# Halved value products in the self-attention, and a last batch whose expert results are written straight to token rows, in a three-part decoder layer on one core

## The reference, cut to what matters

```python
# x: (4, 512, 128) float32, ctx: (4, 154, 128), mask: (4, 1, 512, 154)
x = x + causal_attention(layernorm(x), Wk, Wq, Wv)              # one head of 128
x = x + cross_attention(layernorm(x), ctx, mask, wq, ..., bo)   # 16 heads of 8
x = x + block(layernorm(x))
def block(x):
    q, k, v = (x @ W + b for W, b in ...)                       # 16 heads of 8, rotary on q and k
    ao = softmax(q k^T / sqrt(8)) v                             # full 512 x 512, per head
    x1 = layernorm(x + ao @ Wo + bo) * g1 + be1
    p, e = top_k(softmax(x1 @ Wg + bg), 2)                      # 2 of 8 experts per token
    y = gelu(x1 @ W1[e] + b1[e]) @ W2[e] + b2[e]                # 128 -> 512 -> 128
    return layernorm(x1 + sum(p * y)) * g2 + be2
```

## Time and profile before

| | before |
|---|---|
| median of 3 executions | 735.01 us (733.05 to 737.16) |
| the profiled execution | 731.61 us, span 729.8 us |
| mean granted TensorE clock in it | 0.953 |
| TensorE matmul busy | 639.2 us, 88% |
| VectorE busy | 456.0 us, 62% |
| ScalarE busy | 344.2 us, 47% |
| GpSimd busy | 120.7 us, 17% |

### The profile page before, as it was taken

The page is one execution under the profiler, slowest core; times in us unless marked ns, Lnnn a source line. Parts: engine busy times, 40 slices in busy tenths (PEclk is TensorE's granted clock), DMA queues, the critical chain, the costliest instruction groups (busy, mean ns, idle before and its releaser), DMA issues.

```text
span 729.8 us, 10620 instructions
## 1 busy us (share of the span) xinstructions
PE 639.2 (88%) x3790; PEld 390.5 (54%) x3798; DVE 456.0 (62%) x1119; ACT 344.2 (47%) x617; POOL 120.7 (17%) x121
## 2 busy tenths in 40 slices
PE   4899899998898999999898999999889999887940
PEld 2564454346655753368636643388447533476840
DVE  4673688737934678458826678677436777378303
ACT  0405027773044457765244567763444566542520
POOL 5100100001041100001224200030406000220414
PEclk9999999999989999999999999999999998998985
DMA  6300000001043540003252630021345500036841
GB/s 196 112 0 1 1 0 1 1 1 36 1 149 97 156 135 1 1 1 114 68 169 67 179 98 1 1 57 50 101 144 160 160 0 1 30 96 194 280 109 43
DMA packets 45084, 54.95 MB, mean 75 GB/s; under 512 B 4347, under 2 KB 35433, under 8 KB 45033
## 3 DMA queue, kind: packets, MB, share of 16 engines
q1 hardware_dynamic: 43240, 50.61, 23.8%
q0 software_dynamic: 1792, 3.67, 1.6%
HBM read 46.73 MB, written 7.54 MB: 74 GB/s over the span
## 4 chain that ended last, share of the span: by engine, by line
PE 61%; DVE 22%; issue 6%; ACT 4%; POOL 3%; DMA 2%; SPq 1%; POOLq 0%; ACTq 0%; DVEq 0%
PE banks L1730 9%; PE banks L1371 5%; PE banks L1720 5%; PE banks L1385 5%; PE banks L1699 4%; DVE nm L1203 3%; DVE nm L1139 3%; PE banks L1348 3%; PE banks L1681 3%; PE banks L1622 2%; PE banks L1620 2%; DVE hat L893 2%; PE banks L1639 2%; POOL rstd L566 2%; PE banks L1633 2%
## 5 line engine op out<-in xcount | busy, mean ns | idle before, releaser
L1203 DVE TENSOR_REDUCE nm<-banks 128x1 fp32r<-128x512 f32 x256 | 160.3, 683 | 41.5 <-PE banks L1699 40.4
L846 ACT ACTIVATE px<-banks 128x1024 f32<-128x1024 f32 x128 | 126.4, 1023 | 47.1 <-PE banks L1720 46.7
L674 ACT ACTIVATE hT<-banks,wp 128x128 f32<-128x128 f32 x240 | 68.3, 370 | 78.2 <-PE banks L1371 78.1
L566 POOL TENSOR_TENSOR rstd<-ve,misc 128x4 f32<-128x4 f32 x19 | 19.5, 1027 | 457.9 <-DVE ve L887 457.9
L1699 PE MATMUL banks<-kst,qst 32*128 32x512 f32 x256 | 84.3, 499 | 1.6 <-ACT kst L819 0.8
L1730 PE MATMUL banks<-px,vf 128*32 128x512 f32 x512 | 73.4, 647 | 4.8 <-ACT ot L852 3.1
L1371 PE MATMUL banks<-xT,wp 128*128 128x128 f32 x480 | 69.6, 292 | 7.9 <-DMA wp<-in_experts 4.8
L1371 PEld LDWEIGHTS banks<-xT,wp 128*128 128x128 f32 x480 | 63.0, 203 | 15.3 <-issue 9.7
L1385 PE MATMUL banks<-wp,hT 128*128 128x128 f32 x480 | 67.2, 285 | 2.2 <-ACT hT L674 2.1
L1385 PEld LDWEIGHTS banks<-wp,hT 128*128 128x128 f32 x480 | 62.0, 201 | 3.8 <-ACT hT L674 2.6
L1720 PE MATMUL banks<-q2st,kst 32*128 32x512 f32 x256 | 59.3, 513 | 0.0
(11 more groups left out here) (273 smaller groups left out, 988.9 us busy)
## 6 DMA issues: line engine op xcount, KB each, us to landing
wp<-in_experts SPq DMA_DIRECT2D x60, 514.0 KB, 4.7
b2r<-in_L_ffn_b SPq DMA_DIRECT2D x60, 64.0 KB, 4.3
expert_rows<-xs SPq DMA_DIRECT2D x12, 256.0 KB, 5.2
xs<-expert_tokens SPq DMA_DIRECT2D x9, 256.0 KB, 3.0
msk<-in_mask SPq DMA_DIRECT2D x4, 308.0 KB, 3.0
xin<-in_x SPq DMA_DIRECT2D x4, 256.0 KB, 2.9
ot<-in_const_sel SPq DMA_DIRECT2D x1, 1024.0 KB, 5.3
out<-yg SPq DMA_DIRECT2D x4, 256.0 KB, 2.3
```

The source lines that it names most:

```text
L566: pool.tensor_tensor(rstd[:, n, :], ve[:, n, :], exponent, ALU.pow).then_inc(k[f"ln_rstd{n}"], 1)
L674: ins = act.activation(hT[:, n % 2, c * P:(c + 1) * P], bank[h_bank(p, i)][:, c * P:(c + 1) * P], ACT.Gelu, bias=wp[:, n % WSLOTS, 2 * FF ...
L846: act.activation(px[:, c % 2, 2 * i:2 * i + 2, :], banks[:, 4 + 2 * i:6 + 2 * i, :], ACT.Exp, scale=SCALE_H).then_inc(k["f_exp"], 1)
L1203: dve.tensor_reduce(nm[:, t, g, BLK * hh:BLK * hh + 1], bank[s1_bank(g, t, i)], AX.X, ALU.max, negate=True).then_inc(k["f_max"], 1)
```

## The change

Five edits.

1. `sums_of` takes a range of columns. In the chunks that also have `s1`, from (0, 1) to (2, 2) of every batch, ten in number, the value product is cut into two halves of 256 columns, one behind each pair of `s1`, so 40 products become 80 halves. In chunk 3 of groups 0 and 1 the first half stands before `q2`. The other products stay whole.
2. The 52 `keep_warm` matmuls in `s2` are 256 columns wide and no longer 512.
3. In `cross` of batches 1 to 3, `up(p, 1)` stands before the turn of the normalised rows.
4. Last batch, order: only the first group of tokens is placed before the first tile, the others behind tiles 1, 5 and 9. Three more weight slots lie in `px`, which the attention no longer needs, so eight tiles' weights are loaded ahead. The output store of batch 2 stands behind all of the last batch's weight loads. The last tile's result goes to the bank of the group before, and its bias is added by itself.
5. Last batch, results: three small operations on VectorE and eight indirect writes (`send_ids`, 4 bytes a row) note in memory which token row each slot belongs to. SyncE loads that table (`row_of`). Each tile of the last batch is then written by one indirect write (`send_rows`) from `ysb` to the token rows in `token_rows`: four before `finish(B - 2)`, eleven behind it. `keep_y` and the eight indirect reads go for this batch; four plain loads fetch the rows. The last two passes over the output are folded into the layer norm's (subtract the mean and scale by g2 before the power is there, multiply and add behind it), and the output is stored in two halves.

```diff
+def w_slot(n):
+    i = n - NT * (B - 1)
+    if i < 0:
+        return n % WSLOTS
+    return (*range(WSLOTS, WSLOTS + WMORE), *range(WSLOTS))[i % (WSLOTS + WMORE)]
...
@@ SyncE
-                if n >= WSLOTS:
-                    sp.wait_ge(k["y_part"], n - WSLOTS + 1)
+                if w_free(n):
+                    sp.wait_ge(k["y_part"], w_free(n))
...
-                    for i in range(WSLOTS):
+                    for i in range(YG):
                         load_expert(B - 1, i)
-                for g in range((NT - WSLOTS) // YG, NG):
-                    keep_y(p, g)
-            sp.wait_ge(k["out_ready"], B)
-            sp.dma_start(out[B - 1].rearrange("(t p) d -> p t d", p=P), outb).then_inc(k["out_stored"], 16)
+                    keep_y(p, NG - 2)
+                    for i in range(YG, WSLOTS + WMORE):
+                        load_expert(B - 1, i)
+                    keep_y(p, NG - 1)
+                    sp.wait_ge(k["xs_sent"], 16 * 2 * T * B)
+                    sp.dma_start(row_of[:], row_dram.rearrange("(s i) o -> s (i o)", s=P)).then_inc(k["slots_loaded"], 16)
...
+            for i in range(2):
+                sp.wait_ge(y_sent[i], 16 * sum(min(YG, NT - YG * g) for g in range(i, NG, 2)))
+            for t in range(T):
+                sp.dma_start(yg[:, :, t, :], yt_dram[0:2 * S].rearrange("(j t p) d -> p j t d", j=2, p=P)[:, :, t, :],
+                             ).then_inc(xs_in[t], 16)
...
@@ GpSimd
+            def send_rows(i):
+                g = i // YG
+                n = NG * (B - 1) + g
+                if i == 0:
+                    pool.wait_ge(k["slots_loaded"], 32)
+                if i % YG == 0 or i == NT - 1:
+                    pool.wait_ge(k["y_out"], n + 1 + (i == NT - 1))
+                pool.indirect_dma_start(yt_dram, bass.IndirectOffsetOnAxis(row_of[:, i:i + 1], 0),
+                                        ysb[:, n % 2, i % YG, :], None).then_inc(y_sent[g % 2], 16)
...
-            pool.wait_ge(k["g_slots"], B)
+            send_ids()
             fetch_tokens(B - 2)
+            for i in range(YG):
+                send_rows(i)
             finish(B - 2)
-            fetch_tokens(B - 1)
+            for i in range(YG, NT):
+                send_rows(i)
             rstd_of(4, B - 1)
...
@@ VectorE, add_biases of the last batch
+                    if p == B - 1 and g >= 2:
+                        dve.wait_ge(y_sent[n % 2], 16 * YG)
...
@@ TensorE
-                        keep_warm(1, 4)
+                        keep_warm(1, 4, S // 2)
...
+                            if g * T + c and ga < G:
+                                sums_of(g * T + c - 1, i * S // 2, (i + 1) * S // 2)
                             if c == T - 1 and i == 0 and g + 1 < G:
                                 q2(g + 1)
-                            if g * T + c and i == (ga >= G or c == T - 1):
-                                if g * T + c == 1:
-                                    pe.wait_ge(k["f_v"], b + 1)
-                                sums_of(g * T + c - 1)
+                            if g * T + c and ga >= G and i:
+                                sums_of(g * T + c - 1, 0, S)
...
             place_tokens(0)
-            place_tokens(1)
             for i in range(NT):
                 up(B - 1, i)
                 if i:
                     down(B - 1, i - 1)
-                if i in (YG - 2, 2 * YG - 2):
-                    place_tokens(i // YG + 2)
+                if i in PLACES_BEHIND:
+                    place_tokens(i // YG + 1)
             down(B - 1, NT - 1)
```

More of the change, by code:

```diff
@@ L202, in y_bank, with w_loads, w_free @@
     return Y_BANKS[(g - GROUPS_BEFORE_F) % 2] if p == B - 1 or p == B - 2 and g >= GROUPS_BEFORE_F else Y_BANKS[0]
+def w_slot(n):
[3 more added lines that the diff above has]
+    return (*range(WSLOTS, WSLOTS + WMORE), *range(WSLOTS))[i % (WSLOTS + WMORE)]
+def w_loads(n):
+    return sum(w_slot(m) == w_slot(n) for m in range(n + 1))
+def w_free(n):
+    return max([m + 1 for m in range(n) if w_slot(m) == w_slot(n)], default=0)
 def rank_bank(p):
@@ L387, in build @@
         y_back = [sem(f"y_back{t}") for t in range(T)]
+        y_sent = [sem(f"y_sent{i}") for i in range(2)]
         block = stack.enter_context(nc.Block())
@@ L401, in build, with weights @@
         X_HEAD_BANKS = (4, 1, 2, 3)
+        def weights(n, first, last):
+            i = w_slot(n)
+            if i < WSLOTS:
+                return wp[:, i, first:last]
+            first, last = [S + WP * (i - WSLOTS) + c for c in (first, last)]
+            return px[:].rearrange("p i h s -> p (i h s)")[:, first:last]
         def a_scores(t):
@@ L524, in _ @@
                         load_expert(p, i)
-                for i in range(WSLOTS, NT):
+                ahead = WSLOTS if p < B - 1 else WSLOTS + WMORE
+                for i in range(ahead, NT):
                     load_expert(p, i)
-                    done = i - WSLOTS + 1
-                    if done % YG == 0:
+                    done = i - ahead + 1
+                    if done % YG == 0 and p < B - 1:
                         keep_y(p, done // YG - 1)
@@ L862, in _ @@
                 gelus(B - 2, label)
[L863 to L867 removed]
+            tokens_turned(B - 1, (0,))
+            for i in range(NT):
+                gelus(B - 1, (i,))
+                if i in PLACES_BEHIND:
+                    tokens_turned(B - 1, (i // YG + 1,))
         @block.vector
```

143 lines of the change are left out of this document (99 added, 44 removed).

## The result

| | before | changed |
|---|---|---|
| median of 4 executions each | 734.03 us (731.56 to 737.16) | 710.1 us (704.46 to 713.1) |
| ratio, 95% interval | | 0.967 (0.960 to 0.974) |
| the profiled execution | 731.61 us, span 729.8 | 712.04 us, span 710.2 |
| mean granted TensorE clock in it | 0.953 | 0.958 |
| attention of the four batches | 66.0, 71.2, 70.2, 71.6 | 61.7, 67.2, 69.7, 63.9 |

The attention runs from a batch's first `s1` to its last value product.

What follows compares the result with a forecast made beforehand. TensorE (61% of the chain, VectorE 22%) was taken to bound the kernel, GpSimd's queue its end. Savings of 17.1 + 0.4 + 2.2 + 2.3 + 1.7 = 23.7 us off 735.01 gave 711.3 us; range 703 to 725.

Steps and rivals of the forecast that it cites:

- The halved products: Attention: a half value product is two waves of 0.21 plus 0.14 of filling and emptying, 0.57 us.
- the bounds of 0.43 and 0.99: Limits for a half product: 0.43 us with no filling, 0.99 if as dear as the whole.
- the halves don't get cheaper: Rival, attention: at 0.99 a half, the cut adds 5.5 us in four batches; 736.1 us, chance 0.05.
- The 0.14 behind a product: Attention: filling and emptying the array, 0.14 us, beside a value product's two waves of 512 columns, 0.43 each.
- The attention, 17.1 + 0.4: Self-attention: halves and shorter keep_warm save 17.1 us in four batches, 0.4 more in the fourth batch's last group.
- The clock, 2.2: Fourth batch's attention: three clock falls cost 4.5 us; half of that, 2.2 us, was taken as saved.
- `cross`, 2.3: `cross`: `up(p, 1)` moves into the turn's wait, so projections start 0.79 us earlier in 3 batches, 2.3 us.
- The last batch, 1.7: Last batch: GpSimd's queue ends last, and the span ends at 728.1 for 729.8, 1.7 us less.
- to the end it is 2.7 now: Program's end: from the last pass over the output to the end, 2.7 us, kept for the changed kernel.
- GpSimd's queue gives nothing back: Rival, last batch: GpSimd's queue decides the end, and the stage costs 2.5 us more; 715.5 us, chance 0.20.
- The exponentials take the place of the maxima: Rival, attention: ScalarE comes 0.5 us later, losing 0.3 us 40 times, 12 us; 723.3 us, chance 0.13.
- The clock slower: Rival, attention: halved keep_warm lets the clock fall, 1.5 us each, two in each of 16 groups; 757 us, chance 0.04.

Runs made afterwards that it cites:

- experiment 1: Changed kernel with its value products whole again, keep_warm still at 256 columns: 746.97 us, ratio 0.998 to the kernel before.
- experiment 5: The changed kernel, unedited, run again on another chip beside the kernel before: 726.36 us, ratio 0.973.
- experiment 8: Changed kernel with the last batch's power moved off GpSimd (VectorE's reciprocal, ScalarE's square root): 713.03 us, ratio 0.969 to the kernel before.
- experiment 9: Changed kernel with batch 2's last group stored early and group 1's bias moved behind batch 2's statistics: 706.97 us, ratio 0.966 to the kernel before.
- the first two jobs: Two sets of four follow-up kernels, on two chips, each beside the kernel before, which took 744.5 and 746.5 us there.
- experiment 6 with row writes: Changed kernel with batch 2's last group stored ahead of four of the last batch's weight loads: 724.86 us, ratio 0.969 to the kernel before.
- the third job: The last set of four follow-up kernels, on a third chip, beside the kernel before, which took 730.2 us there.
- 7: Changed kernel with no keep_warm in `s2` (52 matmuls fewer): 721.34 us, ratio 0.963 to the kernel before.

## Why the prediction was right, and where it was not

The time came out at 710.1 for 711.3, the ratio 0.967 for 0.968. The mechanism held: the spacing gave most of it, as experiment 1 shows. But the parts were further off than the sum, and that the sum met the median so closely was luck.

- **The halved products**: 0.57 us each, as worked out; the bounds of 0.43 and 0.99 and the rival "the halves don't get cheaper" are settled. The 0.14 behind a product was right in size, and each half pays it. The Trainium skill (TensorEngine Tiling (Array Packing), Key Properties) has a change of tiling mode drain the array; the trace agrees in that this part does not shrink with the columns, but no run tells a drain from other fixed costs of a product.
- **The attention, 17.1 + 0.4**: too much. At full clock a batch gains 3.0 us: 70.22 us before (third batch, no low clock) and 67.2 with the cut in all later profiles without one. That is 12 in four, not 17. From keep_warm to keep_warm groups 0, 1 and 2 gained 0.8, 1.2 and 1.0 for 1.3, 1.6 and 1.4. The term that was mis-sized is keep_warm, taken at 0.21. It is 0.31 between quarter-array work, and 0.10 in each of four chunks is the whole difference between the 10.7 predicted for group 1 and the 11.12 measured. The rows before had it. The first keep_warm of a batch stands behind a full-array matmul, and there the old one of 512 columns took 424.36 - 424.03 = 0.33, for 0.43 between quarter-array work. At 256 columns it is 0.21 (experiment 5) and 0.31:

```profile
424.03 0.40 PE L1348 MATMUL banks<-sel_r,eye_r 128*128 128x512 f32 x1
424.36 0.50 PE L1720 MATMUL banks<-q2st,kst 32*128 32x512 f32 x2
```
```profile
418.49 0.28 PE L1450 MATMUL banks<-sel_r,eye_r 128*128 128x256 f32 x1
418.70 0.50 PE L1831 MATMUL banks<-q2st,kst 32*128 32x512 f32 x2
```

  So 256 columns are worth 0.12 in either place, and a neighbour of the other tiling mode costs 0.10 at either width. I had halved the whole 0.43, fixed part and all: the mode change was counted for the products and not for keep_warm, which makes two.
- **The clock, 2.2**: half of the falls was a guess between ends. The profile gives more: three falls of 1.5 in the fourth batch gone, 2.1 in the first two batches' last groups (17.18 and 16.97 at a granted clock of 0.90 before, 16.01 at full now), 2.5 lost to the fall in the third: 4.1. The prediction had missed those two falls; it says that the first three batches keep the clock. But experiment 8 has a fall of 24 us in the third batch with the same order, and it costs 8.7. The sign is not the order's alone.
- **`cross`, 2.3**: 0.84 for the 0.79 in the fourth batch. In the other two the turn stood at the low clock before (4.3 and 4.0 us to the projections, 1.9 now), yet from one attention to the next the profile gains 1.5, loses 0.5 and gains 0.9, 1.8 in all: the clock now falls elsewhere in there.
- **The last batch, 1.7**: 0.6. In its own coordinates: first read predicted 47.4 us behind the last value product, measured 48.9; end of batch 2's last pass 69.2, 68.9; last write 83.1, 82.7; VectorE's last operation 94.7, 93.6. The path was right and even 1.1 too dear, though two misses cancel: the first read comes 1.5 late, and from it to the last pass it is 20.0 for 21.8. TensorE, taken to be through 5.5 earlier, is through 76.6 us into the stage for 75.8 before. The wait for its last weights ended as added up (69.7 us into the stage), but the two `up` and three `down` behind it take 6.9 more, for which the sum had no room. GpSimd was later still, so it cost nothing here. The step that failed is its last: "to the end it is 2.7 now". It is 4.95, since the drain of GpSimd, hidden before, comes 1.2 later behind writes and the output lands earlier.
- **The rivals.** GpSimd's queue gives nothing back: true to 0.6 us in the stage, which alone would have been 712.4. The exponentials take the place of the maxima: no. TensorE's whole wait for them ahead of value products is 1.2 us (the page's row of these products, all four batches):

```profile
L1845 PE MATMUL banks<-px,vf 128*32 128x256 f32 (+1 forms) x832 | 78.4, 449 | 2.8 <-ACT px L922 1.2
```

  The clock slower: no, not even with no keep_warm at all, though single long falls cost up to 8.7, and with whole products (experiment 1) one execution had three.

The profiled execution gained 19.6 us of span: 0.6 ahead of the first attention, 16.6 in the four, 1.8 between them, 0.6 in the last stage. The medians gained 24. The other 4.3 lies in executions that were not profiled, and of the changed kernel the profiled one has the lowest granted clock (0.958, the others 0.960 to 0.974, down to 704.46 us). The attention was 5 too high, the clock too low, and the median happened to have what the profile lacks. The terms are what to trust less.

## What to carry to other kernels

Spacing pays where a producer and a consumer trade bursts: cutting one product in two took 1.1 us off a group of 12.2, with no work less, and halving a filler in the same place gave half of what its columns promise, because what it pays for standing between matmuls of another tiling mode (0.10 for each such neighbour) does not shrink with it. When the engine that ends a program is relieved, look at what each engine still does to close; here one instruction on GpSimd at the very end put 2.7 us on the program. And a queue that decides the end is shortened ahead of its first wait: one store moved by four loads, with one VectorE operation out of its way, gave 4.2 us of the last stage. The store alone gave nothing on a chip where TensorE came late to what VectorE waited for; without that lateness it was not tried, and by the profile of experiment 9 it should have given some 3.5 of the 4.2 (an estimate).

## What the runs showed of the hardware that I had not expected

- GpSimd's closing drain ends 4.7 us behind its last instruction where indirect reads came before it (before: 724.5 to 729.1), 5.9 where indirect writes did (704.1 to 710.0). With that instruction moved off the end it is hidden (experiment 8).
- A full-array matmul between quarter-array ones holds the array 0.10 us longer than behind a full-array one: 0.43 for 0.33 at 512 columns, 0.31 for 0.21 at 256.
- In the first two jobs, on two chips, TensorE's signals came up to 10.6 us later than the modelled ends of its matmuls (experiment 6 with row writes: products through at 666.8, ScalarE's copy at 677.5), in dense stretches, most of them expert products. The last stage took 102.8 for 98.5 there, and with the last batch of before 106.6 for 99.1. In the first profiles and in the third job there is none of it.
- The granted clock can stay low for 24 us in an attention that holds it elsewhere (417.5 to 441.4 in experiment 8, 260.9 to 284.8 in 7, three times in the profile of 1): two groups then take 16.1 and 16.6 us for 12.96 and 11.12 (in 8).
